# Images 0 to 3 combined among the last expert tiles, and the pair sum of the others done by TensorE as it turns them

## Chip, cores and metric

The kernel runs on one core of a Trainium2 chip. The metric is the device time of one execution in microseconds (us); the median of the runs is compared.

## The reference, cut to what matters

The input is 16 images of 128 channels by 28 x 28 places. A convolution block and a spiking attention block come first. Their result `t` has 16 x 784 = 12,544 tokens of 128 channels, and then a mixture of experts is added:

```python
top_vals, top_idx = jax.lax.top_k(flat @ Wr, 2)        # flat: layer norm of t, 12544 x 128
top_w = softmax(top_vals)
gates = zeros(N, 8).at[arange(N)[:, None], top_idx].add(top_w)
for e in range(8):
    hdn = gelu(flat @ W1[e] + b1[e])                   # 128 -> 512
    out = out + gates[:, e:e+1] * (hdn @ W2[e] + b2[e])  # 512 -> 128
x = from_tokens(t + out)                               # back to channels x places
```

So every token has two chosen experts, and its result is the sum of two gated expert rows and of `t`, turned from token rows into channel rows.

## The kernel before, in words

**First stage (to about 390 us).** Images go through convolution, attention and routing. For each token two rows are sent to a table in HBM, sorted by expert. The sum `t` of each image stays in SBUF (`t2_all`).

**Tile loop (to about 696 us).** The table is worked off in 105 tiles of 256 rows (`TILES`). Every engine runs its own loop over the tiles; semaphores order them.

- SP (`load_tile`, issue L464 and L467) loads tile t turned (`xrt`, four slots) and its routing fields. It waits until the hidden layer of tile t-4 is done, so a load is issued three tiles ahead of its use.
- TensorE runs `hidden(t + 2)` (L943, 24 products into `pair_b` or `pair_c`, in two halves) and then `output(t)` (L957 and L960, into `pair_d`).
- ScalarE runs `gelu` (L1152), which reads the PSUM half and writes a float32 copy `g` in SBUF (in `seen_g`), and `high_half` (L1159), which rounds `g` to float16.
- VectorE runs `gated` (L1656: output times gate into `y`), every fourth tile `fields` (L1631 to L1634), and `split` (L1640: `g` minus its float16 half, two pieces a tile). `output(t)` waits for both pieces of `split(t)`. `hidden(t + 2)` waits for the two `gelu` halves of tile t, which have then left the PSUM pair free.
- POOL (`store_tile`, L678) scatters the 256 gated rows of a tile to the table `expert_rows` in HBM, by two indirect DMAs of 128 rows. `y` has room for 16 tiles, so POOL may run late.

**Combination (from about 696 us).** For each of 16 images:

- SP loads the two expert rows of every token (`load_y`, L481, 784 KB), into 8 buffers in turn. The first six are issued after the last `load_tile` and after a wait for the stores of tiles 0 to 87 (`KNOWN`), which hold all rows of images 0 to 12. Images 13 to 15 wait for all stores.
- VectorE adds the two rows (`sum_rows`, L1697).
- TensorE turns the sum by seven transposes (`turn_sum`, L995).
- VectorE adds `t` (`add_rows`, L1703) and writes `o` (four buffers, in `seen_g`, over `g`).
- ScalarE's queue sends `o` to the output (L1192, 392 KB an image). `add_rows(i)` waits until the output of image i-4 has landed.

Of the kernel before, what the change touches and what calls it, by code (L numbers as in the profile page):

```python
# [33 lines left out]
P = 128  # L34
# [67 lines left out]
def build(nc, a, out):  # L102
# [7 lines left out]
    with ExitStack() as ctx:  # L110
# [61 lines left out]
        def part(words):  # L172
# [50 lines left out]
        xrt = sb("xrt", [P, DEEP, 2, TILE], F16)  # L223
        g = seen_g[:, 0:4 * FC * TILE].bitcast(F32).rearrange("p (u f k) -> p u f k", u=2, f=FC)
        ghl = xb_x1[:, 0:2 * FC * TILE].bitcast(F16).rearrange("p (u h k) -> p u h k", u=2, h=2)
# [11 lines left out]
        fetched = p1_area[0:TT, :].rearrange("p (u t k d) -> p u t k d", u=FETCHED, t=NT, k=2)  # L237
        later = w1_place[0:TT, 0:(ROW_BUFFERS - FETCHED) * 2 * NT * P].rearrange("p (u t k d) -> p u t k d", u=ROW_BUFFERS - FETCHED, t=NT, k=2)
        ysum = w2_place[0:TT, 0:SUM_DEEP * NT * P].rearrange("p (u t d) -> p u t d", u=SUM_DEEP, t=NT)
        o = seen_g[:, 0:2 * SUM_DEEP * L].bitcast(F32).rearrange("p (u l) -> p u l", u=SUM_DEEP)  # L240
# [16 lines left out]
            "dest_ready", "y_ready", "y_copied", "stored_0", "stored_1", "stored_2", "stored_3",  # L257
            "yl_loaded_0", "yl_loaded_1", "yl_loaded_2", "yl_loaded_3", "yl_loaded_4", "yl_loaded_5", "yl_loaded_6", "yl_loaded_7", "ysum_ready", "yt_ready", "o_ready", "out_0", "out_1", "out_2", "out_3",
        )}

        def rows_of(i):

            b = i % ROW_BUFFERS
            return fetched[:, b] if b < FETCHED else later[:, b - FETCHED]

# [79 lines left out]
        def mean_place(n):  # L345

            pair = (pb, pc, pd, pd)[n // 2]
            return pair[:, n % 2 * BANK:(n % 2 + 1) * BANK]

        def score_pair(t):  # L350
# [4 lines left out]
        def _(sp):  # L355
# [121 lines left out]
            def load_y(i):  # L477

                if some(i + 1 - ROW_BUFFERS):
                    sp.wait_ge(S["ysum_ready"], i + 1 - ROW_BUFFERS)  # L480
                sp.dma_start(rows_of(i).rearrange("p t k d -> p (t k d)"), y_img[i]).then_inc(S[f"yl_loaded_{i % ROW_BUFFERS}"], 16)  # L481

# [18 lines left out]
            for b in range(STORE_BATCHES):  # L501
                sp.wait_ge(S[f"stored_{b}"], 32 * store_uses(b, KNOWN))
            for i in range(FETCHED):
                load_y(i)
            sp.wait_ge(S["h_ready"], 2 * TILES)
            for i in range(FETCHED, EARLY_IMAGES):
                load_y(i)
            for b in range(STORE_BATCHES):
                sp.wait_ge(S[f"stored_{b}"], 32 * store_uses(b))
            for i in range(EARLY_IMAGES, IMAGES):  # L510
                load_y(i)


# [179 lines left out]
        def _(pe):  # L693
# [240 lines left out]
            def hidden(t):  # L934
                w0 = experts[t] * HID
                hp, slot = (pb, pc)[t % 2], t % DEEP

                if some(2 * (t - 1)):
                    pe.wait_ge(S["g_ready"], 2 * (t - 1))
                pe.wait_ge(S[f"xrt_loaded_{slot}"], 16 * (t // DEEP) + 16)  # L940
                for f in range(FC):
                    for m, (wp, xp) in enumerate(((0, 0), (0, 1), (1, 0))):
                        last = T.matmul(hp[:, f * TILE:(f + 1) * TILE], w1[:, wp, bass.ds(w0 + f * P, P)],  # L943
                                        xrt[:, slot, xp, :], start=(m == 0), stop=(m == 2))
                    if f % GELU_HALF == GELU_HALF - 1:
                        last.then_inc(S["h_ready"], 1)
# [19 lines left out]
            def take_experts(t, count):  # L966
# [3 lines left out]
                experts.update(zip(range(t, t + count), table(mybir.EngineType.PE, tile_w, t, count, E - 1)))  # L970

            take_experts(0, TAKE)
# [17 lines left out]
            def turn_sum(i):  # L990
                if some(i + 1 - SUM_DEEP):
                    pe.wait_ge(S["o_ready"], i + 1 - SUM_DEEP)
                pe.wait_ge(S["ysum_ready"], i + 1)
                for t in range(NT):
                    last = T.transpose(psum[i % SUM_DEEP][:, t * P:t * P + TT], ysum[:, i % SUM_DEEP, t, :], ident[0:TT, 0:TT])  # L995
                last.then_inc(S["yt_ready"], 1)

            for i in range(IMAGES):
                turn_sum(i)
# [3 lines left out]
        def _(act):  # L1003
# [137 lines left out]

            def half_of(tensor, t, h):
                return tensor[:, t % 2, GELU_HALF * h:GELU_HALF * (h + 1), :].rearrange("p f k -> p (f k)")

            def gelu(t):
                hp = (pb, pc)[t % 2]
                if some(2 * (t - 1)):
                    act.wait_ge(S["ghl_ready"], 2 * (t - 1))
                for h in range(2):

                    act.wait_ge(S["h_ready"], 2 * t + h + 1)
                    A.activation(half_of(g, t, h), hp[:, h * BANK:(h + 1) * BANK], ACT.Gelu, scale=1.0 / WSCALE).then_inc(S["g_ready"], 1)  # L1152

            def high_half(t):
                if some(t - 1):
                    act.wait_ge(S["y_ready"], t - 1)
                for h in range(2):
                    act.wait_ge(S["g_ready"], 2 * t + h + 1)
                    A.activation(ghl[:, t % 2, 0, h * 2 * TILE:(h + 1) * 2 * TILE], half_of(g, t, h), ACT.Copy).then_inc(S["g_hi_ready"], 1)  # L1159

# [28 lines left out]

            for i in range(IMAGES):  # L1190
                act.wait_ge(S["o_ready"], i + 1)
# [6 lines left out]
        def _(dve):  # L1198
# [444 lines left out]
            def gv(t, h):  # L1643
                return g[:, t % 2, 2 * h:2 * h + 2, :].rearrange("p f k -> p (f k)")

# [4 lines left out]
            def gated(t):  # L1650
                slot, (q, half) = t % DEEP, batch_of(t)
                dve.wait_ge(S["y_ready"], t + 1)
                if slot == 0:
                    dve.wait_ge(S["gate_ready"], q + 1)
                b0 = (t % 2) * BANK
                V.tensor_tensor(y[:, t % STORE_DEEP, :, :], pd[:, b0:b0 + 2 * P].rearrange("p (s c) -> p s c", s=2),  # L1656
                                bc_last(share[:, half, slot, :], P), ALU.mult).then_inc(S["y_copied"], 1)

            fields(0, 0)
# [3 lines left out]
            for t in range(TILES):  # L1663
# [29 lines left out]
            def sum_rows(i):  # L1693
                if some(i + 1 - SUM_DEEP):
                    dve.wait_ge(S["yt_ready"], i + 1 - SUM_DEEP)
                dve.wait_ge(S[f"yl_loaded_{i % ROW_BUFFERS}"], 16 * (i // ROW_BUFFERS) + 16)
                V.tensor_tensor(ysum[:, i % SUM_DEEP, :, :], rows_of(i)[:, :, 0, :], rows_of(i)[:, :, 1, :], ALU.add).then_inc(S["ysum_ready"], 1)  # L1697

            def add_rows(i):
                dve.wait_ge(S["yt_ready"], i + 1)  # L1700
                if some(16 * (i // SUM_DEEP)):
                    dve.wait_ge(S[f"out_{i % SUM_DEEP}"], 16 * (i // SUM_DEEP))
                V.tensor_tensor(o[:, i % SUM_DEEP, :].rearrange("p (q t) -> p t q", t=NT), psum[i % SUM_DEEP][:, 0:NT * P].rearrange("p (t k) -> p t k", k=P)[:, :, 0:TT],  # L1703
                                t2_all[:, i * L:(i + 1) * L].rearrange("p (t k) -> p t k", k=TT), ALU.add).then_inc(S["o_ready"], 1)

            dve.wait_ge(S["t2_kept_0"], 32 * PAIRS)
            dve.wait_ge(S["t2_kept_1"], 32 * PAIRS)
            for i in range(SUM_AHEAD):
                sum_rows(i)
            for i in range(IMAGES):  # L1710
                if i + SUM_AHEAD < IMAGES:
                    sum_rows(i + SUM_AHEAD)
                add_rows(i)

# [22 lines left out]
```

## Time and profile before

| what | us |
|---|---|
| runs | 753.41, 750.35, 753.29 (median 753.29) |
| the profiled execution, its own time | 751.24 |
| its span, first to last instruction | 749.5 |
| TensorE busy in the span | 626.6 (84%) |
| VectorE, ScalarE, POOL busy | 571.1, 486.2, 464.6 |

The rows further down come from this one profiled execution. A timeline row gives the start, the duration, the engine, the line, the operation and what it writes and reads; a bracket says how long the engine was idle before and what ended that. "x7" means that seven records are merged in one row; a float32 product makes two records, a float32 transpose one.

### The profile page before, as it was taken

The numbers are of one execution on the slowest core, as the hardware profiler recorded it, in microseconds if no ns is written. First come the engines' busy times: TensorE is split into PE (matmuls) and PEld (weight loads), VectorE is DVE, ScalarE is ACT, GpSimd is POOL, SyncE is SP. The second block draws the span as 40 slices with busy tenths as digits, with TensorE's granted clock in tenths as the row PEclk, the third lists the DMA queues.
The fourth block names the chain that finished last, engine by engine and source line by source line (L and its number), as shares of the span: only waits on it lengthen the run. The fifth ranks groups of instructions, "written<-read, shape, count | busy, mean of one in ns | idle before, by whom it ended". The sixth has DMA issues, their size and how long they took to land.

```text
span 749.5 us, 20954 instructions
## 1 busy us (share of the span) xinstructions
PE 626.6 (84%) x6696; PEld 493.1 (66%) x6696; DVE 571.1 (76%) x1757; ACT 486.2 (65%) x940; POOL 464.6 (62%) x476
## 2 busy tenths in 40 slices
PE   1577879888888898889749899999999999999533
PEld 1244555555555555555529898989999999999423
DVE  6567978999998899999767778656666666666867
ACT  1256757777876677877638777777777777777000
POOL 7000025666666576577777677777777777777720
PEclk9988978999999999999859999999999999999755
DMA  5754484655555555552245344564444454447996
GB/s 142 216 153 127 118 204 127 178 178 163 165 154 162 166 178 179 150 166 95 67 107 97 80 95 95 118 132 90 100 101 93 101 102 95 90 99 195 328 343 263
DMA packets 138771, 108.85 MB, mean 145 GB/s; under 512 B 100339, under 2 KB 121367, under 8 KB 138674
## 3 DMA queue, kind: packets, MB, share of 16 engines
q1 hardware_dynamic: 121874, 75.13, 40.2%
q0 software_dynamic: 13056, 26.02, 11.8%
q10 hardware_dynamic: 3744, 6.43, 2.5%
q8 instruction: 58, 0.95, 0.5%
q14 instruction: 39, 0.32, 0.2%
HBM read 45.26 MB, written 42.85 MB: 118 GB/s over the span
## 4 chain that ended last, share of the span: by engine, by line
PE 45%; DVE 23%; DMA 14%; ACT 6%; issue 5%; SPq 4%; POOL 2%; DVEq 0%; POOLq 0%; ACTq 0%
PE pair_d L960 16%; PE pair_b L943 8%; PE pair_c L943 7%; DMA conv_planes<-conv_y 6%; DMA out<-seen_g 5%; PE pair_a L741 3%; DMA conv_y<-conv_planes 3%; DVE xb_x L1640 3%; DVE p_area L1387 2%; PE pair_c L827 2%; ACT p_area L1051 2%; PE pair_d L957 2%; DVE w L1467 1%; DVE st L1314 1%; SPq L411 1%
## 5 line engine op out<-in xcount | busy, mean ns | idle before, releaser
L678 POOL DMA_INDIRECT expert_rows<-conv_y,dest x210 | 226.6, 1079 | 67.5 <-issue 58.6
L607 POOL DMA_INDIRECT dispatched_rows<-p_area,pos x198 | 198.9, 1005 | 110.3 <-issue 54.4
L960 PE MATMUL pair_d<-w,xb_x 128*128 x2520 | 168.2, 220 | 0.0
L1159 ACT ACTIVATE xb_x<-seen_g 128x512 f16<-128x512 f32 x210 | 120.8, 624 | 61.7 <-PE pair_d L960 59.8
L960 PEld LDWEIGHTS pair_d<-w,xb_x 128*128 128x128 f16 x2520 | 152.3, 98 | 2.5
L1640 DVE TENSOR_TENSOR xb_x<-seen_g,xb_x 128x512 f16<-128x512 f32 x210 | 135.7, 688 | 22.2 <-ACT xb_x L1159 20.2
L1656 DVE TENSOR_TENSOR conv_y<-pair_d,share 128x256 f32<-128x256 f32 x105 | 44.5, 424 | 70.6 <-PE pair_d L960 68.4
L741 PE MATMUL pair_a<-conv_y,p_area 128*32 128x392 f16 x1152 | 64.7, 366 | 20.8 <-DMA conv_y<-conv_planes 15.7
L943 PE MATMUL pair_b<-xrt,w 128*128 128x256 f16 x636 | 79.4, 275 | 2.3 <-issue 2.3
L943 PE MATMUL pair_c<-xrt,w 128*128 128x256 f16 x624 | 78.3, 276 | 0.0
L600 POOL TENSOR_TENSOR conv_y<-conv_y 128x784 f16<-128x784 f32 x16 | 26.0, 1625 | 73.2 <-ACT conv_y L1030 73.0
L943 PEld LDWEIGHTS pair_b<-xrt,w 128*128 x636 | 60.4, 99 | 8.9 <-issue 2.4
L943 PEld LDWEIGHTS pair_c<-xrt,w 128*128 x624 | 59.9, 99 | 6.8
L741 PEld LDWEIGHTS pair_a<-conv_y,p_area 128*32 128x32 f16 x1152 | 29.9, 104 | 42.8 <-issue 27.1
L1152 ACT ACTIVATE seen_g<-pair_b 128x512 f32<-128x512 f32 x106 | 56.7, 585 | 1.7 <-PE pair_b L943 1.1
L1152 ACT ACTIVATE seen_g<-pair_c 128x512 f32<-128x512 f32 x104 | 55.5, 584 | 0.0
L957 PE MATMUL pair_d<-b,two_rows 128*128 x210 | 46.2, 220 | 4.9 <-DVE xb_x L1640 4.5
L1077 ACT ACTIVATE seen_g<-pair_a 112x784 bf16<-112x784 f32 (+2 forms) x48 | 30.6, 638 | 25.6 <-PE pair_a L817 25.1
L1051 ACT ACTIVATE p_area<-pair_b,shift,rstd 112x128 f32<-112x128 f32 x112 | 40.9, 469 | 5.7 <-DVE shift L1348 5.6
L1077 ACT ACTIVATE seen_g<-pair_c 112x672 bf16<-112x672 f32 (+1 forms) x64 | 30.2, 471 | 16.4 <-PE pair_c L817 16.4
L797 PE MATMUL pair_c<-w_t,p_area 128*112 128x128 f32 x224 | 29.6, 286 | 10.8 <-ACT p_area L1067 9.5
L797 PEld LDWEIGHTS pair_c<-w_t,p_area 128*112 128x112 f32 x224 | 26.7, 185 | 16.7 <-DVE p_area L1387 14.2
(264 smaller groups left out, 1094.1 us busy)
## 6 DMA issues: line engine op xcount, KB each, us to landing
conv_y<-conv_planes SPq DMA_DIRECT2D x64, 225.0 KB, 3.9
xb_x<-in_x SPq DMA_DIRECT2D x32, 392.0 KB, 4.4
p_area<-expert_rows SPq DMA_DIRECT2D x12, 784.0 KB, 17.0
conv_planes<-conv_y SPq DMA_DIRECT2D x32, 225.0 KB, 5.1
t_all<-p_area SPq DMA_DIRECT2D x16, 392.0 KB
out<-seen_g ACTq DMA_DIRECT2D x16, 392.0 KB, 9.4
t_all<-in_L_ffn_W SPq DMA_DIRECT2D x16, 256.0 KB, 4.9
expert_rows<-conv_y,dest POOLq DMA_INDIRECT x210
```

The costliest lines, as they stand in the source:

```text
L607: pool.indirect_dma_start(xs, bass.IndirectOffsetOnAxis(ap=pos[0:m, u, t, k:k + 1].bitcast(U32), axis=0), rows[0:m, u, t, :].bitcast(U32), ...
L678: pool.indirect_dma_start(ys, bass.IndirectOffsetOnAxis(ap=dest[:, place, slot, s:s + 1].bitcast(U32), axis=0), y[:, t % STORE_DEEP, s, :] ...
L741: last = T.matmul(pa[g * GROUP_CHANNELS:(g + 1) * GROUP_CHANNELS, h * BANK:h * BANK + HALF], tap_w[:, g, tap, :], stacked_rows[:, u, g, ky ...
L797: last = T.matmul(pc[0:TT, t * P:(t + 1) * P], xt[:, t * TT:(t + 1) * TT], w_t[:, 2, :], start=True, stop=True)
L943: last = T.matmul(hp[:, f * TILE:(f + 1) * TILE], w1[:, wp, bass.ds(w0 + f * P, P)], xrt[:, slot, xp, :], start=(m == 0), stop=(m == 2))
L957: T.matmul(dst, two_rows[:], b2[:, bass.ds(c0, P)], start=True, stop=False)
L960: last = T.matmul(dst, ghl[:, t % 2, gp, f * TILE + s * P:f * TILE + (s + 1) * P], w2[:, wp, bass.ds(w0 + f * P, P)], start=False, stop=(f ...
L1051: last = A.activation(xn[:, t, :], pb[0:TT, t * P:(t + 1) * P], ACT.Identity, scale=rstd[0:TT, t:t + 1], bias=shift[0:TT, t:t + 1])
L1077: A.activation(seen[:, t * L + t * TT:(t + 1) * L], score_pair(t)[0:TT, 0:L - t * TT], ACT.Sign).then_inc(S["seen_ready"], 1)
L1152: A.activation(half_of(g, t, h), hp[:, h * BANK:(h + 1) * BANK], ACT.Gelu, scale=1.0 / WSCALE).then_inc(S["g_ready"], 1)
L1159: A.activation(ghl[:, t % 2, 0, h * 2 * TILE:(h + 1) * 2 * TILE], half_of(g, t, h), ACT.Copy).then_inc(S["g_hi_ready"], 1)
L1640: V.tensor_tensor(ghl[:, t % 2, 1, h * 2 * TILE:(h + 1) * 2 * TILE], gv(t, h), ghl[:, t % 2, 0, h * 2 * TILE:(h + 1) * 2 * TILE], ALU.subt ...
```

## The change

- `gelu` writes its result back into the PSUM half that it read (`hidden_half`), and `high_half` and `split` read it there; `g` in SBUF is gone. So `hidden(t)` now waits, half by half, for `split(t - 2)` in place of `gelu(t - 2)`.
- SP issues the row loads of images 0 to 6 among its tiles 96 to 102, after a wait for the stores of tiles 0 to 87 at its tile 96. Eleven row buffers take the place of eight.
- Images 0 to 3 are combined inside the tile loop: `sum_rows(i)` on VectorE at the end of tile 92 + 3i, `turn_sum(i)` on TensorE after the output of tile 94 + 3i, `add_rows(i)` on VectorE in two parts, at the ends of tiles 94 + 3i (4 of the 7 columns) and 96 + 3i (3 of 7). SP sends their outputs.
- For images 4 to 15 VectorE's `sum_rows` is gone. TensorE makes 14 float32 products an image in place of 7 transposes: each of the two row blocks times the identity, accumulated in PSUM.

```diff
-FETCHED, ROW_BUFFERS = 6, 8
-SUM_DEEP, SUM_AHEAD = 4, 2
+FETCHED = 6
+ROW_BUFFER_OF = (0, 1, 2, 3, 4, 5, 6, 0, 1, 2, 3, 7, 8, 9, 10, 4)
+SUM_DEEP, SUM_HALF = 4, 4
+COMBINED, COMBINE_AT, COMBINE_EVERY = 4, 92, 3
+FETCH_AT, FETCHED_AMONG = 96, 7
...
# SP, in its loop over the tiles, and after it
                 load_tile(t)
+                if t == FETCH_AT:
+                    for b in range(STORE_BATCHES):
+                        sp.wait_ge(S[f"stored_{b}"], 32 * store_uses(b, KNOWN))
+                if FETCH_AT <= t < FETCH_AT + FETCHED_AMONG:
+                    load_y(t - FETCH_AT)
+            for i in range(COMBINED):
+                sp.wait_ge(S["yt_ready"], i + 1)
+                load_y(FETCHED_AMONG + i)
+                if i < COMBINED - 1:
+                    store_out(i)
...
# TensorE
-                if some(2 * (t - 1)):
-                    pe.wait_ge(S["g_ready"], 2 * (t - 1))
                 for f in range(FC):
+                    if f % GELU_HALF == 0 and some(2 * (t - 2) + 1):
+                        pe.wait_ge(S["ghl_ready"], 2 * (t - 2) + f // GELU_HALF + 1)
...
+                    for t in range(NT):
+                        for k in range(2):
+                            last = T.matmul(sum_pair(i)[:, t * P:t * P + TT], rows_of(i)[:, t, k, :], ident[0:TT, 0:TT], start=(k == 0), stop=(k == 1))
...
                 output(t)
+                for i in range(COMBINED):
+                    if t == COMBINE_AT + COMBINE_EVERY * i + 2:
+                        turn_sum(i)
...
# ScalarE
-                    A.activation(half_of(g, t, h), hp[:, h * BANK:(h + 1) * BANK], ACT.Gelu, scale=1.0 / WSCALE).then_inc(S["g_ready"], 1)
+                    A.activation(hidden_half(t, h), hidden_half(t, h), ACT.Gelu, scale=1.0 / WSCALE).then_inc(S["g_ready"], 1)
...
# VectorE
-                    V.tensor_tensor(ghl[:, t % 2, 1, h * 2 * TILE:(h + 1) * 2 * TILE], gv(t, h),
+                    V.tensor_tensor(ghl[:, t % 2, 1, h * 2 * TILE:(h + 1) * 2 * TILE], hidden_half(t, h),
...
+                    if t == at:
+                        sum_rows(i)
+                    if t == at + 2:
+                        add_rows(i, 0, SUM_HALF)
+                    if t == at + 4:
+                        add_rows(i, SUM_HALF, NT)
```

## Rows read from the trace of the kernel before

**Rows 1.** Windows of 10 us after the tile loop, and one inside it (columns in the first line).

```profile
core 0: us, PE busy (x) PEld busy (x) DVE busy (x) ACT busy (x) POOL busy (x), PEclk, DMA share, GB/s
655.00:682.00 27.00, 27.00 (x367) 25.34 (x365) 17.13 (x41) 20.31 (x41) 21.18 (x20) 1.00 0.47 97
690.00:700.00 10.00, 7.47 (x101) 6.54 (x98) 7.15 (x15) 2.91 (x7) 7.87 (x8) 1.00 1.02 309
...
720.00:730.00 10.00, 3.79 (x18) 2.81 (x16) 7.23 (x6) 0.00 (x0) 0.00 (x0) 0.50 1.03 354
```

**Rows 2.** Chain of waits after the tile loop: start us, us, what.

```profile
712.75 14.88 DMA out<-seen_g
```

**Rows 3.** TensorE's last tiles in order of time (start us, us, engine, line).

```profile
686.58 1.47 PE L943 MATMUL pair_c<-xrt,w 128*128 128x256 f16 x12
...
689.34 1.47 PE L943 MATMUL pair_b<-xrt,w 128*128 128x256 f16 x12
...
695.61 0.83 PE L960 MATMUL pair_d<-w,xb_x 128*128 x12
```

**Rows 4.** VectorE in one late tile and in the combination, in order of time.

```profile
684.68 1.30 DVE L1640 TENSOR_TENSOR xb_x<-seen_g,xb_x 128x512 f16<-128x512 f32 x2 [0.24 <-ACT xb_x L1159]
...
704.65 1.58 DVE L1703 TENSOR_TENSOR seen_g<-pair_c,t_all 128x784 f32<-128x784 f32 x1
706.08 1.07 DVE L1697 TENSOR_TENSOR w<-p_area 112x896 f32<-112x896 f32 x1
...
745.08 1.54 DVE L1703 TENSOR_TENSOR seen_g<-pair_d,t_all 128x784 f32<-128x784 f32 x1
```

**Rows 5.** Float32 work of TensorE in the first stage, in order of time.

```profile
292.45 1.40 PE L850 MATMUL pair_d<-wr_c,p_area 128*128 128x8 f32 x12
293.71 0.37 PE L852 MATMUL pair_d<-wr_c,rests 128*128 128x8 f32 x2
...
302.32 0.89 PE L771 MATMUL pair_b<-ident,p_area 112*128 112x112 f32 x7
303.14 0.88 PE L741 MATMUL pair_a<-conv_y,p_area 128*32 128x392 f16 x16
305.00 1.75 PE L797 MATMUL pair_c<-w_t,p_area 128*112 128x128 f32 x14 [0.98 <-ACT p_area L1067]
306.59 0.19 PE L860 MATMUL pair_b<-chosen,before 128*128 128x64 bf16 x1
```

**Rows 6.** TensorE around 416 us, after its longest wait, in order of time.

```profile
416.72 0.23 PE L957 MATMUL pair_d<-b,two_rows 128*128 x1 [1.99 <-DVE xb_x L1640]
416.83 1.39 PE L960 MATMUL pair_d<-w,xb_x 128*128 x12
...
419.40 2.10 PE L943 MATMUL pair_c<-xrt,w 128*128 128x256 f16 x12
```

**Rows 7.** TensorE's waits in the tile loop: us in total, times, longest us.

```profile
PE pair_d L957 <- DVE xb_x L1640: 3.8, 5, 2.0
```

**Rows 8.** Groups by line and shape: VectorE over PSUM and SBUF, 512 wide.

```profile
L1461 DVE TENSOR_TENSOR t_all<-t_all,pair_d 127x512 f32<-127x512 f32 x4 | 2.7, 684 | 3.1 <-PE pair_d L723 3.1
```

**Rows 9.** POOL's stores of expert rows, in order of time.

```profile
668.59 1.05 POOL L678 DMA_INDIRECT expert_rows<-conv_y,dest  x1 [0.30 <-issue]
...
704.88 0.97 POOL L678 DMA_INDIRECT expert_rows<-conv_y,dest  x1 [0.30 <-issue]
706.16 1.83 POOL L678 DMA_INDIRECT expert_rows<-conv_y,dest  x1 [0.30 <-issue]
```

**Rows 10.** VectorE's gated copy of tile 87.

```profile
650.40 0.42 DVE L1656 TENSOR_TENSOR conv_y<-pair_d,share 128x256 f32<-128x256 f32 x1 [0.23 <-PE pair_d L960]
```

**Rows 11.** SP's queue: the last load of tile 96, the first of tile 97.

```profile
658.77 0.38 SPq L467 DMA_DIRECT2D fld<-dispatched_rows  x1
660.07 2.02 SPq L464 DMA_TRANSPOSE xrt<-dispatched_rows  x1
```

**Rows 12.** DMA issues from 655 to 682 us: KB each, median us to landing.

```profile
p_area<-expert_rows SPq DMA_DIRECT2D x1, 784.0 KB, 6.6
```

More of the change, by code:

```diff
@@ L970, in take_experts, with turn_sum @@
                 experts.update(zip(range(t, t + count), table(mybir.EngineType.PE, tile_w, t, count, E - 1)))
+            def turn_sum(i):
+                if i <= COMBINED:
+                    if some(i):
+                        pe.wait_ge(S["o_ready"], i)
+                elif i < COMBINED + SUM_DEEP:
+                    if i == COMBINED + SUM_DEEP - 1:
+                        pe.wait_ge(S["y_copied"], TILES)
+                else:
+                    pe.wait_ge(S["o_ready"], i + 1 - SUM_DEEP)
+                if i < COMBINED:
+                    pe.wait_ge(S["ysum_ready"], i + 1)
+                    for t in range(NT):
+                        last = T.transpose(sum_pair(i)[:, t * P:t * P + TT], rows_of(i)[:, t, 0, :], ident[0:TT, 0:TT])
+                else:
+                    pe.wait_ge(S[f"yl_loaded_{ROW_BUFFER_OF[i]}"], loads_of(i))
+                    for t in range(NT):
+                        for k in range(2):
+                            last = T.matmul(sum_pair(i)[:, t * P:t * P + TT], rows_of(i)[:, t, k, :], ident[0:TT, 0:TT], start=(k == 0), stop=(k == 1))
+                last.then_inc(S["yt_ready"], 1)
             take_experts(0, TAKE)
@@ L987, in _ @@
                 output(t)
[L990 to L998, printed above, removed]
+                for i in range(COMBINED):
+                    if t == COMBINE_AT + COMBINE_EVERY * i + 2:
+                        turn_sum(i)
+            for i in range(COMBINED, IMAGES):
                 turn_sum(i)
@@ L1187, in _ @@
                     gate_tanh(q, half)
-            for i in range(IMAGES):
+            for i in range(COMBINED, IMAGES):
                 act.wait_ge(S["o_ready"], i + 1)
@@ L1657, in gated, with sum_rows, add_rows, combine_early @@
                                 bc_last(share[:, half, slot, :], P), ALU.mult).then_inc(S["y_copied"], 1)
+            def sum_rows(i):
+                dve.wait_ge(S[f"yl_loaded_{ROW_BUFFER_OF[i]}"], loads_of(i))
+                V.tensor_tensor(rows_of(i)[:, :, 0, :], rows_of(i)[:, :, 0, :], rows_of(i)[:, :, 1, :], ALU.add).then_inc(S["ysum_ready"], 1)
+            def add_rows(i, t0, t1):
+                if t0 == 0:
+                    dve.wait_ge(S["yt_ready"], i + 1)
+                    if some(16 * (i // SUM_DEEP)):
+                        dve.wait_ge(S[f"out_{i % SUM_DEEP}"], 16 * (i // SUM_DEEP))
+                last = V.tensor_tensor(o[:, i % SUM_DEEP, :].rearrange("p (q t) -> p t q", t=NT)[:, t0:t1], sum_pair(i)[:, 0:NT * P].rearrange("p (t k) -> p t k", k=P)[:, t0:t1, 0:TT],
+                                       t2_all[:, i * L:(i + 1) * L].rearrange("p (t k) -> p t k", k=TT)[:, t0:t1], ALU.add)
+                if t1 == NT:
+                    last.then_inc(S["o_ready"], 1)
+            def combine_early(t):
+                if t == COMBINE_AT:
+                    dve.wait_ge(S["t2_kept_0"], 32 * PAIRS)
+                    dve.wait_ge(S["t2_kept_1"], 32 * PAIRS)
+                for i in range(COMBINED):
+                    at = COMBINE_AT + COMBINE_EVERY * i
+                    if t == at:
[4 more added lines that the diff above has]
+                        add_rows(i, SUM_HALF, NT)
             fields(0, 0)
@@ L1690, in _ @@
                     gate(q, half)
[L1693 to L1713, printed above, removed]
+                combine_early(t)
+            combine_early(TILES)
+            for i in range(COMBINED, IMAGES):
+                add_rows(i, 0, NT)
 _INS = ["x"] + ["L0_conv_" + n for n in ("dw_w", "dw_b", "bn1_g", "bn1_b", "bn1_m", "bn1_v", "pw_w", "pw_b", "bn2_g", "bn2_b", "bn2_m", "bn2_v")] \
```

52 lines of the change are left out of this document (28 added, 24 removed).

## The prediction

> **What bounds the kernel now.** I read the windows first: which engine is full in which stretch, then the clock and the DMA share. In the tile loop TensorE is busy all the time (27.00 of 27.00 us) at the full granted clock, with the DMA engines at 0.47. After the loop this turns round: the DMA share is 1.02 to 1.03, TensorE does under 4 us of work in ten, and its granted clock falls to 0.50, the 1.2 GHz level [rows 1]. Next the chain: its long pieces after the loop are three waits for output transfers, the longest 14.88 us [rows 2]. So there are two stages with two limits: a tile loop set by TensorE, in which 0.53 of the DMA time is unused, and a combination set by transfers. The loop's last product ends at 695.61 + 0.83 = 696.44 us [rows 3]. To the end of the span (749.5 us) that leaves **53.1 us** for the combination.
>
> **The change, part by part.** The sum is made against the profiled execution: 751.24 us, with a span of 749.5. It is 2.05 us below the median of the runs, so I work out the difference and subtract that from 753.29.
>
> *Transfers.* Seven of 16 row loads and the first outputs move into the loop. Of the tail's transfers, about six loads and 13 outputs are left: at the tail's 309 GB/s [rows 1] a load of 803 KB takes 2.6 us and an output of 401 KB 1.3 us, together 33 us. That is less than TensorE's new work below, so TensorE is late next.
>
> *Turning with the sum (images 4 to 15).* Seven transposes become 14 float32 products, 28 records an image. No row shows this shape, so I bound it. Records that hardly stream and are set by loading 128 columns came at (293.71 - 292.45) / 12 = 0.105 us; records that stream 128 columns at (306.59 - 305.00) / 14 = 0.114; transposes of 112 columns, with the same operands, at (303.14 - 302.32) / 7 = 0.117 [rows 5]. The new ones load 128 and stream 112, nearest to the first: I take 0.11, that is 3.08 us an image and **37.0 us** for twelve (35.3 to 39.3). VectorE's 1.54 us an image [rows 4] lies beside it. After the loop's last output TensorE first waits for image 3's second part, since image 4 uses its PSUM pair: start of the gated copy 0.2, copy 0.42 [rows 10], three sevenths of the 1.54 us add with its fixed part 0.75, together about 1.4 us. Behind the last product come one add (1.54 and 0.2 to start) and what now follows the last add, 749.5 - 745.08 - 1.54 = 2.9 us [rows 4]. New tail: 1.4 + 37.0 + 1.7 + 2.9 = 43.0 us, **10.1 us less**.
>
> *Combining images 0 to 3 in the loop.* Each turn takes TensorE 0.82 us [rows 5], on the path: 3.3 us. VectorE has the time: in a tile its pieces are 0.42 and 1.30 us of 2.76 (689.34 - 686.58) [rows 3, 4, 10], and one pair sum (1.07) or half add (0.96 or 0.75) follows. But turn i waits for the second half add of image i - 1, which VectorE reaches only behind that tile's gated copy and split; with the pair sum of the tile before pushing it by some 0.3 us I get waits of 0.3 us (image 1) and 0.7 (image 2, whose tile has the fields too). At the end, from the end of output 101, VectorE runs copy, split, pair sum 3, copy, fields, split, half add: 6.2 us. TensorE is through its products after 4.2 us, waits 2.0, turns image 3 (0.8) and does the last output (1.45): 8.6 us where it was 696.44 - 689.34 = 7.1. So 3 x 0.82 + 1.0 + 1.5 = **5.0 us more**.
>
> *GELU in place.* ScalarE and VectorE now read or write PSUM. For the split the nearest row is a VectorE subtraction of 512 columns of PSUM from SBUF: 684 ns [rows 8], against 1.30 / 2 = 0.65 for a piece now; I take no change. ScalarE writing to PSUM stands in no row; ScalarE is idle for a quarter of the loop [rows 1], so between 0.3 us less and 0.3 more a tile it is covered; I take zero. The new wait of `hidden` for the split: the split that starts at 684.68 has its first piece ready at 685.33, and the product that would wait for it starts at 686.58 [rows 3, 4]. That cover is 1.25 us; VectorE's insertions use 0.3 to 0.5 of it. It fails only where VectorE is already late: five waits, 3.8 us in all [rows 7]. There `hidden` waits too, which before ran in the shadow of the wait, for about 0.5 us more; but VectorE or a field load, not TensorE, sets the time in these places, so they don't add up: **0.5 us more** (0 to 2.5).
>
> *The clock.* After its longest wait, 1.99 us, TensorE ran slower for some 4 us: 12 products took 1.39 us for 0.83, 12 others 2.10 for 1.47 [rows 3, 6]. Both output halves and the hidden layer together, that cost 1.8 us. The 2.0 us wait near the end is like it: **1.8 us more** (0 to 1.8). After that the products follow each other without gaps, as in the first stage.
>
> *POOL and SP.* SP's wait at tile 96 stands ahead of the tile loads that feed TensorE, so it counts. Before, tile 87's rows are ready at 650.82 us but POOL begins to store them at 668.59: 17.8 us late [rows 9, 10]. A store takes 0.97 us and 0.30 between two, so 2.55 us a tile, less than TensorE's 2.76: POOL should catch up, and doesn't. Why: a store that began at 706.16, inside VectorE's pass over two SBUF tiles (706.08 to 707.15), took 1.83 us; one that began inside a pass over PSUM and SBUF (704.65) took 0.97 [rows 4, 9]. The split is now of the first kind, and becomes one of the second. Gaining 0.21 us a tile over some 71 tiles, POOL makes up about 15 us and is 3 us late at tile 87: stores issued by 656.4, and landed before or just after SP asks, at 659.2 [rows 11]. The first row load takes 6.6 us [rows 12]; VectorE wants it near 666.6. So zero.
>
> The Trainium skill, "SBUF — State Buffer", section "Who interferes with whom", has two sentences here: a VectorE instruction with two SBUF inputs contends with a GpSimd instruction that reads SBUF, but a tensor-tensor pass should not hold up descriptor generation (marked there as inferred). By the second, the split never delayed POOL and the lag stays. The rows of 1.83 and 0.97 us speak against that; rival one is what it would give.
>
> **Sum:** -10.1 + 5.0 + 0.5 + 1.8 = **-2.8 us**, that is 748.4 on the profiled run, and **750.5** from the median.
>
> **Rivals.**
> 1. *SP's wait for stored rows (slower).* If POOL stays 17.8 us late, SP stands until 668.59 + 2.6, about 671, not 659.2. The first row load lands at 677.6; VectorE stands at pair sum 0 until then, and after 1.07 + 0.42 + 0.2 + 0.65 us the hidden layer of tile 97 starts at 680.0, not 670.0 (689.34 - 7 x 2.76). Price 10 us: **760.5**. It decides from a lag of about 9 us on. For it: the lag has held over the loop. Against it: the two rows above.
> 2. *Turned tiles late behind row loads.* Both go through SP's queue. A tile uses 0.47 x 2.76 = 1.3 us of DMA time, a load 2.6: 3.9 us in a period of about 3.05 with the turns. After seven, 3.9 + 6 x 0.85 = 9 us are queued, with some 2 us to land, against 670.0 - 660.07 = 9.9 us from a tile's load to its use. Price 0 to 5 us, say 3: **753.5**, no change.
> 3. *Half clock through the whole tail.* 12 images at twice 3.08 us: 37 us more, **787.5**. Against it: unbroken float32 work, which the first stage did at the full rate.
> 4. *TensorE better than taken.* 0.105 a record, no fall of the clock, no early waits: 1.7 + 1.8 + 0.5 less, **746.5**.
>
> **Chances and range.** A difference of 0.5%, 3.8 us, is about what a measurement can tell from none. The forecast with rival 4 as its lower end has 0.72 (its own range 745 to 755), rival 1 0.12, rival 2 0.12, rival 3 0.04. Of the 0.72 the part below 749.5 is 0.42, as the forecast lies only 1 us above that line and its bounds reach 4 below; 0.28 is no change, 0.02 slower. Rival 2 gives 0.07 and 0.05. So faster 0.42, same 0.35, slower 0.23. The range, with run scatter of 1.5 us, is 744.5 to 757.5, which leaves out rivals 1 and 3 at their full price.
>
> **What would show it.** Right: the granted clock stays at 1.00 in most of the tail; 28 records an image in about 3.1 us back to back, and output waits gone from the chain; stores no slower than about 1 us, POOL done a few us after the last tile; the end of the loop at 702 to 704 us. Wrong: TensorE idle before the hidden layer of tiles 97 to 104 with a load or the split as releaser; float32 records of 0.2 us; splits well over 0.7 us; the chain in the tail still on transfers.

## The result, and the profile after

The changed kernel took 756.75 us (median of 20 runs, 751.70 to 764.93) against 750.09 for the kernel before, run beside it (20 runs, 742.22 to 760.27). The ratio is 1.0104, 95% interval 1.0076 to 1.0132: about 1% slower. The forecast was 750.5 us, and most likely faster or no change. That 756.75 still lies inside the range (to 757.5) is luck: the forecast started from a median of three runs, 753.29, and the 20 runs of the same kernel give 3.2 us less. Taken from 750.09, the same sum gives 747.3 and a range to 754.3. What follows is about why the sign was wrong. The ratios are of fast runs: a run more than 1.5% above the fastest of its kernel counts as slow and is left out, and so are the stage times of `behind_fields_half_tail`, whose profile was taken in such a run.

The profiled execution took 754.19 us with a span of 752.5, and 751.24 and 749.5 before. Two events divide it: the first product of the tile loop and the last. In time order, TensorE, the loop's first product before, then after:

```profile
388.59 2.74 PE L943 MATMUL pair_b<-xrt,w 128*128 128x256 f16 x12 [2.27 <-issue]
```

```profile
386.70 2.74 PE L975 MATMUL pair_b<-xrt,w 128*128 128x256 f16 x12 [2.25 <-issue]
...
708.21 0.83 PE L992 MATMUL pair_d<-w,xb_x 128*128 x12
710.22 3.38 PE L1021 MATMUL pair_a<-ident,p_area 112*128 112x112 f32 x28 [1.18 <-DVE seen_g L1706]
713.44 3.29 PE L1021 MATMUL pair_b<-ident,p_area 112*128 112x112 f32 x28
...
744.70 3.29 PE L1021 MATMUL pair_d<-ident,p_area 112*128 112x112 f32 x28
```

Before, the loop ended at 696.44 [rows 3]. So:

| profiled execution, us | before | after | difference | forecast |
|---|---|---|---|---|
| before the loop | 388.59 | 386.70 | -1.9 | 0 |
| tile loop | 307.85 | 322.34 (to 708.21 + 0.83) | **+14.5** | +7.3 |
| combination behind it | 53.06 | 43.46 | **-9.6** | -10.1 |
| span | 749.5 | 752.5 | +3.0 | -2.8 |

The change does not touch what comes before the loop; the 1.9 us there are taken as scatter between executions. The combination did what was forecast. The loop lost twice as much as forecast, and there lies the error.

The same windows as [rows 1], after:

```profile
655.00:682.00 27.00, 23.91 (x302) 22.27 (x300) 16.20 (x35) 15.88 (x34) 15.57 (x16) 0.94 1.01 219
...
712.00:722.00 10.00, 10.00 (x92) 10.00 (x91) 4.80 (x3) 0.00 (x0) 0.69 (x1) 1.00 1.02 276
...
732.00:742.00 10.00, 10.00 (x92) 10.00 (x91) 5.00 (x4) 0.00 (x0) 0.00 (x0) 1.00 0.55 215
```

Behind the loop TensorE is now full at a granted clock of 1.00 (it was under four tenths, at 0.50), and it bounds that stage. In the loop's end TensorE has lost 3.1 of 27 us, and the DMA share has gone from 0.47 to 1.01. The chain of waits names what it stood for, the landing of two field loads:

```profile
668.23 7.32 DMA fld<-dispatched_rows
...
684.42 8.02 DMA fld<-dispatched_rows
```

VectorE waits for these fields, and TensorE for VectorE's split behind them (VectorE first, then TensorE, in order of time):

```profile
675.65 0.17 DVE L1672 TENSOR_TENSOR mine<-fld,tile_expert 128x8 f32<-128x8 f32 x1 [4.77 <-DMA fld<-dispatched_rows]
...
692.54 0.17 DVE L1672 TENSOR_TENSOR mine<-fld,tile_expert 128x8 f32<-128x8 f32 x1 [4.34 <-DMA fld<-dispatched_rows]
```

```profile
676.95 1.60 PE L975 MATMUL pair_b<-xrt,w 128*128 128x256 f16 x12 [3.09 <-DVE xb_x L1681]
...
681.11 1.73 PE L975 MATMUL pair_c<-xrt,w 128*128 128x256 f16 x12
...
693.84 1.48 PE L975 MATMUL pair_b<-xrt,w 128*128 128x256 f16 x12 [3.34 <-DVE xb_x L1681]
```

`fields(q)` runs on VectorE between the gated copy of tile 4q - 2 and the split of tile 4q. SP issues the field load of the batch's last tile, 4q + 3, at the earliest when the hidden layer of tile 4q - 1 is done. VectorE wants it some 3 us later: 668.23 to 675.65 - 4.77 = 670.88 is 2.65 us, and 684.42 to 692.54 - 4.34 = 688.20 is 3.78. Among row loads of 784 KB those 3 KB took 7 to 8 us. SP's queue around the first of them, the row load of image 2 and the field load:

```profile
666.16 0.47 SPq L498 DMA_DIRECT2D p_area<-expert_rows  x1
...
668.23 0.40 SPq L486 DMA_DIRECT2D fld<-dispatched_rows  x1
```

The two waits of TensorE are 6.4 us. The products behind the first were slow, at a mean granted clock of 0.65, that is in part at the lower of its two levels: from one hidden layer to the next it took 681.11 - 676.95 = 4.16 us, not 2.76, and the next was 0.26 late too, together 1.7. Behind the second wait, the longer one, the granted clock was 1.00 and the first twelve products took the usual 1.48 us.

### The profile page after: what moved, and what is told of

It reads as the page before. It is cut to its first block, busy times and chain, and to the rows that moved or that the text cites. A ratio compares the mean times of both kernels' runs of the same rounds, so it can differ in the third digit from the quotient of the medians.

```text
span 752.5 us, 21336 instructions
## 1 busy us (share of the span) xinstructions
PE 644.3 (86%) x6948; PEld 514.2 (68%) x6948; DVE 559.9 (74%) x1749; ACT 480.8 (64%) x940; POOL 443.1 (59%) x476
## 3 DMA queue, kind: packets, MB, share of 16 engines
q0 software_dynamic: 13056, 26.02, 11.9%
## 4 chain that ended last, share of the span: by engine, by line
PE 46%; DVE 26%; DMA 9%; ACT 6%; issue 5%; SPq 4%; POOL 2%; DVEq 0%; POOLq 0%; ACTq 0%
PE pair_d L992 15%; PE pair_b L975 8%; PE pair_c L975 7%; DMA conv_planes<-conv_y 4%; DMA fld<-dispatched_rows 3%; PE pair_a L773 3%; DVE xb_x L1681 2%; DVE p_area L1428 2%; DMA conv_y<-conv_planes 2%; DVE st L1348 2%; PE pair_c L859 2%; ACT p_area L1098 1%; DVE st L1355 1%; PE pair_d L989 1%; DVE w L1508 1%
## 5 line engine op out<-in xcount | busy, mean ns | idle before, releaser
L710 POOL DMA_INDIRECT expert_rows<-conv_y,dest x210 | 204.8, 975 | 86.8 <-issue 55.9
L1200 ACT ACTIVATE xb_x<-pair_b 128x512 f16<-128x512 f32 x106 | 57.6, 595 | 39.0 <-PE pair_d L992 38.2
L1200 ACT ACTIVATE xb_x<-pair_c 128x512 f16<-128x512 f32 x104 | 56.5, 596 | 31.5 <-PE pair_d L992 29.5
L1681 DVE TENSOR_TENSOR xb_x<-pair_b,xb_x 128x512 f16<-128x512 f32 x106 | 68.1, 683 | 10.4 <-ACT xb_x L1200 10.4
L1681 DVE TENSOR_TENSOR xb_x<-pair_c,xb_x 128x512 f16<-128x512 f32 x104 | 66.9, 685 | 9.2 <-ACT xb_x L1200 8.6
L1193 ACT ACTIVATE pair_b<-pair_b 128x512 f32<-128x512 f32 x106 | 58.0, 589 | 3.0 <-PE pair_b L975 2.8
L1193 ACT ACTIVATE pair_c<-pair_c 128x512 f32<-128x512 f32 x104 | 56.4, 584 | 1.1 <-PE pair_c L975 1.0
L1124 ACT ACTIVATE seen_g<-pair_a 112x784 bf16<-112x784 f32 (+2 forms) x48 | 30.6, 638 | 21.9 <-PE pair_a L849 21.5
```

Source lines behind the costliest of these rows:

```text
L710: pool.indirect_dma_start(ys, bass.IndirectOffsetOnAxis(ap=dest[:, place, slot, s:s + 1].bitcast(U32), axis=0), y[:, t % STORE_DEEP, s, :] ...
L1124: A.activation(seen[:, t * L + t * TT:(t + 1) * L], score_pair(t)[0:TT, 0:L - t * TT], ACT.Sign).then_inc(S["seen_ready"], 1)
L1193: A.activation(hidden_half(t, h), hidden_half(t, h), ACT.Gelu, scale=1.0 / WSCALE).then_inc(S["g_ready"], 1)
```

## The experiments

Each ratio is to runs of the kernel before on the same chip.

| run | ratio to before, 95% interval | loop, us | behind it, us |
|---|---|---|---|
| before (profiled) | 1 | 307.85 | 53.06 |
| the change | 1.0104 [1.0076, 1.0132] | 322.34 | 43.46 |
| rows_behind_fields | 0.9959 [0.9921, 0.9997] | 311.91 | 43.46 |
| rows_on_act | 1.0262 [1.0188, 1.0335] | 327.56 | 43.38 |
| gelu_in_place_alone | 1.0029 [0.9983, 1.0075] | 310.64 | 53.27 |
| tail_on_vector | 0.9989 [0.9944, 1.0034] | 321.05 | 38.04 |
| spare_loads_each_tile | 1.0149 [1.0075, 1.0222] | 319.73 | 53.87 |
| spare_loads_behind_fields | 1.0021 [0.9972, 1.0070] | 311.16 | 54.64 |
| behind_fields_vector_tail | 0.9899 [0.9827, 0.9971] | 313.71 | 39.11 |
| behind_fields_half_tail | 0.9869 [0.9794, 0.9943] | - | - |
| before_fields_first | 0.9965 [0.9934, 0.9997] | 306.58 | 51.58 |
| fields_first | 0.9937 [0.9895, 0.9980] | 315.56 | 43.45 |
| fields_first_vector_tail | 0.9851 [0.9805, 0.9896] | 315.68 | 36.40 |
| fields_first_spaced_rows | 0.9871 [0.9820, 0.9921] | 311.46 | 37.91 |

Loop and rest are of the one profiled execution of each run (first hidden product to the end of the last output product, and from there to the end of the span), the ratio is of all its runs. Whole runs of one kernel scatter by 1 to 2%. The loop scatters less: three pairs of runs with the same loop (the change and `tail_on_vector`, `rows_behind_fields` and `behind_fields_vector_tail`, `fields_first` and `fields_first_vector_tail`) differ in it by 1.3, 1.8 and 0.1 us, so a difference under 2 us is read as none.

### Where the row loads stand in SP's queue

```diff
-                if FETCH_AT <= t < FETCH_AT + FETCHED_AMONG:
-                    load_y(t - FETCH_AT)
+                for i in ROWS_AT.get(t, ()):
+                    load_y(i)
...
+ROWS_AT = {95: (0,), 96: (1,), 99: (2,), 100: (3,), 103: (4,), 104: (5, 6)}
```

> The changed kernel, with the row loads of images 0 to 6 issued by SP at its tiles 95, 96, 99, 100, 103 and 104 (one, one, one, one, one, two) in place of one at each of the tiles 96 to 102, so that none stands ahead of the last two tile loads of a batch of four. Queue theory (the fields of tiles 99 and 103 land 7.3 and 8.0 us after their issue because row loads are ahead of them, and cost 3.1 and 3.3 us of TensorE time and 1.9 us of slower clock): fields land in under 4 us there, both stalls go, 6 to 9 us less than the changed kernel, ratio to the kernel before 0.998 to 1.003. In-place theory (the time goes to the hidden layer's new wait for the split and to VectorE's added passes): the stalls stay whatever the order of the loads, ratio 1.008 to 1.012.

The loop fell from 322.34 to 311.91 us, more than the 6 to 9 us that the queue theory gave. VectorE's waits for fields from 600 to 720 us, the change first, then this run:

```profile
DVE mine L1672 <- DMA fld<-dispatched_rows: 10.6, 5, 4.8
```

```profile
DVE mine L1673 <- DMA fld<-dispatched_rows: 1.5, 3, 0.7
```

The longest is 0.7 us, no longer 4.8, although the transfers stayed as dense (columns as in [rows 1], in a window of 40 us):

```profile
650.00:690.00 40.00, 39.99 (x539) 37.70 (x537) 31.44 (x62) 29.03 (x58) 27.14 (x28) 1.00 1.01 218
```

TensorE is full (39.99 of 40 us) at a DMA share of 1.01. So the early fetch need not cost field stalls, and the place of the loads decides. (They are also spread over ten tiles here and not seven; `fields_first`, below, leaves them at one a tile.) But is it their place in SP's queue, or in time? Next, the seven loads left SP's queue for ScalarE's, which issues them in its own loop, behind the work of its tiles 93 to 99.

```diff
+                if FETCH_AT - 5 <= t < FETCH_AT - 5 + FETCHED_AMONG:
+                    n = t - FETCH_AT + 5
+                    act.dma_start(rows_of(n).rearrange("p t k d -> p (t k d)"), ys.rearrange("(b p r) d -> b p (r d)", b=IMAGES, p=TT)[n]).then_inc(S[f"yl_loaded_{ROW_BUFFER_OF[n]}"], 16)
```

> The changed kernel, with the seven row loads among the tiles issued from ScalarE's queue, one behind each of its tiles 91 to 97, in place of SP's. The same bytes at about the same times, on another queue. If it is the order within SP's queue that delays the fields: they land in under 4 us, both stalls go, 6 to 9 us less than the changed kernel. If it is the DMA engines' time, whatever the queue: fields still land after 6 us or more and 0 to 3 us are saved. In-place theory: no difference from the changed kernel.

```profile
670.96 12.30 DMA fld<-dispatched_rows
...
692.68 7.54 DMA fld<-dispatched_rows
```

The kernel got slower still, its loop 5.2 us longer, where 0 to 3 us less were expected. With SP's queue free of row loads, a field load took 12.30 us to land. So the delay needs no row load ahead of it in that queue: large loads in flight from another queue do it as well. By what mechanism inside the DMA engines is not shown.

### The disputed cost by itself

The kernel before, with seven spare loads of 784 KB from `x` into the row buffers, long before these are needed.

```diff
                 load_tile(t)
+                for n in SPARE_LOADS.get(t, ()):
+                    sp.dma_start(fetched[:, n % FETCHED].rearrange("p t k d -> p (t k d)"), a["x"].rearrange("(n b) c h w -> n (b c h w)", b=2)[n].rearrange("(p r) -> p r", p=TT)).then_inc(S["spare_loads"], 16)
...
+SPARE_LOADS = {t: (t - 64,) for t in range(64, 71)}
```

> The kernel before, with nothing of the change in it but the disputed cost by itself: seven loads of 784 KB from the input x into the row buffers (which nobody needs at that time), one behind each of the tiles 64 to 70 in SP's queue, as the changed kernel has its row loads behind tiles 96 to 102. Theory (a field load queued among such loads takes 7 to 8 us and is wanted after some 3): two waits of VectorE for fields of 4 to 5 us each appear, at the batches of tiles 68 and 72, TensorE then waits some 3 us each time, and runs slow for a while behind it; the span grows by 6 to 9 us and the time by about 1%. Rival (the stalls of the changed kernel come from the combination in the loop, which makes VectorE late, and the loads only show beside it): no wait for fields above 1 us here, span and time as before within 1.5 us.

In order of time, VectorE's waits, then TensorE's:

```profile
584.91 0.17 DVE L1635 TENSOR_TENSOR mine<-fld,tile_expert 128x8 f32<-128x8 f32 x1 [4.56 <-DMA fld<-dispatched_rows]
...
602.35 0.17 DVE L1635 TENSOR_TENSOR mine<-fld,tile_expert 128x8 f32<-128x8 f32 x1 [6.40 <-DMA fld<-dispatched_rows]
```

```profile
586.81 0.29 PE L961 MATMUL pair_d<-b,two_rows 128*128 x1 [2.85 <-DVE xb_x L1644]
...
604.25 0.28 PE L961 MATMUL pair_d<-b,two_rows 128*128 x1 [4.69 <-DVE xb_x L1644]
```

Nothing of the change is in this kernel, and the two stalls are there, at the places that the theory gives, the first of the size it gives and the second larger. The loop is 11.9 us longer, the time 1.5%, more than the 6 to 9 us and 1% expected.

```diff
-SPARE_LOADS = {t: (t - 64,) for t in range(64, 71)}
+SPARE_LOADS = {63: (0,), 64: (1,), 67: (2,), 68: (3,), 71: (4,), 72: (5,), 75: (6,)}
```

> The same seven loads of 784 KB in the kernel before, but behind tiles 63, 64, 67, 68, 71, 72 and 75, so that none is in SP's queue in the two tiles ahead of a batch's last fields. Theory: no wait for fields above 1 us, span as before within 1.5 us, although the same 5.6 MB pass through the same engines in about the same time. Rival (the bytes themselves cost the time, by whatever order): the span grows by as much as in the run with one load behind each tile.

The windows of the two, this one second, have nearly the same rate of bytes (230 and 216 GB/s), but TensorE 32.16 and 39.91 us busy of 40:

```profile
565.00:605.00 40.00, 32.16 (x406) 29.58 (x404) 19.04 (x43) 22.66 (x46) 31.17 (x30) 0.94 1.09 230
```

```profile
565.00:605.00 40.00, 39.91 (x544) 37.54 (x541) 25.73 (x55) 30.49 (x60) 31.10 (x30) 1.00 1.06 216
```

One field load was late by 2.65 us here as well, and TensorE by 0.94, so the bound of 1 us was too tight. It was issued 0.43 us ahead of a spare load (602.74) and still took 5.28 us, so a place behind the last fields is no guarantee:

```profile
602.31 5.28 DMA fld<-dispatched_rows
```

The profiled loop is 3.3 us longer than before, but the ratio can't be told from 1. So the bytes alone cost at most a small part of the time.

### The parts of the change

GELU in place without anything else (the hunks of `hidden`, `gelu`, `high_half` and `split` on the kernel before):

```diff
-                    A.activation(half_of(g, t, h), hp[:, h * BANK:(h + 1) * BANK], ACT.Gelu, scale=1.0 / WSCALE).then_inc(S["g_ready"], 1)
+                    A.activation(hidden_half(t, h), hidden_half(t, h), ACT.Gelu, scale=1.0 / WSCALE).then_inc(S["g_ready"], 1)
```

> The kernel before with one part of the change: GELU writes back into PSUM, and the hidden layer waits for the split of two tiles earlier. Queue theory: TensorE waits 1 to 3 us more in the loop's first quarter and nothing later; POOL's stores take 0.98 us at most on average and end a few us after the last tile in place of 21 us after it, so that the last three images load earlier; ratio 0.993 to 1.003. In-place theory: 5 to 8 us more in the loop, ratio 1.005 to 1.010.

No difference that the runs can tell (1.0029, interval on both sides of 1); in the profiled loop it is 2.8 us more. TensorE's waits from 383 to 712 us, before ([rows 7] has a shorter window) and in this run:

```profile
PE pair_d L957 <- DVE xb_x L1640: 4.5, 6, 2.0
```

```profile
PE pair_b L947 <- DVE xb_x L1641: 5.6, 5, 2.1
...
PE pair_d L961 <- DVE xb_x L1641: 1.1, 2, 0.8
```

What it does to POOL stands alone here. The group of stores, the kernel before and this one:

```profile
L678 POOL DMA_INDIRECT expert_rows<-conv_y,dest x210 | 226.6, 1079 | 67.5 <-issue 58.6
```

```profile
L682 POOL DMA_INDIRECT expert_rows<-conv_y,dest x210 | 205.6, 979 | 76.2 <-issue 59.8
```

A store is 0.1 us shorter, and POOL ends 5.6 us after the loop in place of 21.9, with GELU's result in PSUM as the only edit. That edit takes an operand of VectorE's split out of SBUF, but also what ScalarE's `gelu` wrote and `high_half` read. The trace of before has a store that separates them: the one at 693.32 us took 1.19 us, inside the last split (692.98 to 694.27), when the last GELU had ended at 691.66. Next, the change with its pair sums of images 4 to 15 back on VectorE and seven transposes an image:

```diff
-            for i in range(COMBINED, IMAGES):
-                add_rows(i, 0, NT)
+            for i in range(COMBINED, COMBINED + 2):
+                sum_rows(i)
+            for i in range(COMBINED, IMAGES):
+                if i + 2 < IMAGES:
+                    sum_rows(i + 2)
+                add_rows(i, 0, NT)
```

> The changed kernel, with the pair sums of images 4 to 15 on VectorE again (1.07 us each, two images ahead) and seven transposes an image on TensorE. If TensorE's products are what bounds the changed tail (12 x 3.13 = 37.5 us): VectorE's 12 x (1.07 + 1.56) = 31.6 us or the transfers' 33 us bound it now, 2 to 5 us less than the changed kernel. If transfers bound both: no difference within 1 us. The loop and its two stalls are the same in both.

The combination falls from 43.46 to 38.04 us, and the time with it (0.9989 for 1.0104), while the loop keeps its stalls. The two longest pieces of the chain behind the loop are waits for output transfers again, and TensorE is at half clock, with VectorE busy for 9.53 of 10 us:

```profile
706.32 13.43 DMA out<-seen_g
...
721.42 9.70 DMA out<-seen_g
```

```profile
720.00:730.00 10.00, 4.94 (x23) 4.02 (x24) 9.53 (x8) 0.00 (x0) 0.00 (x0) 0.50 1.01 270
```

So what shortened the combination is that seven loads and four images had moved into the loop, not the products with the identity. These made it 5.4 us longer than it need be: a bound of 43 us in place of one of 38.

### Versions that beat both

The edits of `rows_behind_fields` and `tail_on_vector` together:

> The changed kernel with the row loads behind the last fields of a batch, and with the pair sums of images 4 to 15 on VectorE and seven transposes an image on TensorE, as before the change. Theory (the two gains have different places and add up: the loop's end near 699 us, the tail 38 us): span about 737 us, some 5 us under the run with the rows behind the fields alone, time about 0.988 of the kernel before. Rival (in that run the tail is bounded by transfers, and since fewer of them ran in the loop's end or all start later, the tail gets longer as the loop gets shorter): span 740 to 743, no better than either alone.

0.9899 (interval below 1), 742.2 us of span where 737 was forecast: the loop was 313.71 and not 311.9, the combination 39.11 and not 38, and the rest of the difference lies ahead of the loop. The two gains add up, less some 3 us.

> As the run before it, but only images 5, 7, 9, 11 and 13 are summed on VectorE; the other seven of images 4 to 15 are summed by TensorE's products with the identity. Theory A (with all sums on VectorE the tail is set by output transfers, some 33 us of them and more with their waits): relieving VectorE gives nothing, span within 1.5 us of the run with all sums on VectorE. Theory B (there VectorE's 2.6 us an image, or the half clock of the transposes, sets it): TensorE needs 7 x 3.13 + 5 x 1.2 = 28 us, VectorE 12 x 1.54 + 5 x 1.07 = 24 us, and the tail falls from 38 to about 35 us, the span to some 734 us.

```diff
+SUMMED = (5, 7, 9, 11, 13)
...
-                if i < COMBINED:
+                if i < COMBINED or i in SUMMED:
```

Here some images keep the products. The ratios are 0.9869 and 0.9899, each within the other's interval: no gain that the runs can tell, which fits theory A and does not settle it.

Since the place behind the last fields is no guarantee (5.28 us, above), the next runs give the fields more time. The four field loads of a batch are issued with its first tile:

```diff
-                sp.dma_start(fld[:, half, slot, :, :], xs16[bass.ds(tiles_at[t], TILE), 2 * P:ROW].bitcast(F32).rearrange("(s p) c -> p s c", p=P)).then_inc(S[f"fields_{half}"], 16)
+                for n in range(min(DEEP, TILES - t) if slot == 0 else 0):
+                    sp.dma_start(fld[:, half, n, :, :], xs16[bass.ds(tiles_at[t + n], TILE), 2 * P:ROW].bitcast(F32).rearrange("(s p) c -> p s c", p=P)).then_inc(S[f"fields_{half}"], 16)
```

> The kernel before, with one change in SP's queue: the four field loads of a batch (3 KB each) are issued together behind the first tile of the batch, not one behind each tile. VectorE wants all four about three tiles later, so the last of them has some 11 us to land and not 3. Theory (the fields are late because the last one is issued only 3 us ahead of its use): the waits of VectorE for fields, 6 to 7 us over the loop of before, fall under 2 us, TensorE's waits for the split fall from 4.5 to 1 or 2 us, and the span is 2 to 5 us shorter. Rival (the waits of the loop's beginning come from VectorE's other work, the fields only show beside them): waits of TensorE and span as before within 1.5 us.

In the kernel before, the waits for fields (6.5 us in all there) are gone entirely, but TensorE's waits for the split are not:

```profile
PE pair_d L958 <- DVE xb_x L1641: 4.2, 6, 2.0
```

The rival holds here: the waits early in the loop were not for fields. The loop is 1.3 us shorter, the time 0.35% less.

> The changed kernel with the same edit, its row loads still one behind each of the tiles 96 to 102. Theory (it is the short time between a field load and its use that makes the row loads cost anything): no wait for fields above 1 us near the row loads although these stand where they stood; TensorE's two waits of 3.1 and 3.3 us and the slow stretch behind the first are gone, the loop is 8 to 12 us shorter, span 741 to 744. Rival (row loads delay the turned tiles or the stores too, and TensorE would next wait for those): the loop is less than 4 us shorter, and TensorE waits for xrt.

In the changed kernel VectorE has no wait for fields left, with the row loads where the change puts them, one a tile: it was the short slack of the fields, and not how close the row loads stand, that made the field stalls. The loop is 6.8 us shorter, less than the 8 to 12 expected (span 748.9 for 741 to 744), since the next late thing appears, the turned tiles:

```profile
681.61 1.48 PE L976 MATMUL pair_b<-xrt,w 128*128 128x256 f16 x12 [0.49 <-DMA xrt<-dispatched_rows]
686.65 1.48 PE L976 MATMUL pair_c<-xrt,w 128*128 128x256 f16 x12 [1.98 <-DMA xrt<-dispatched_rows]
694.48 1.48 PE L976 MATMUL pair_c<-xrt,w 128*128 128x256 f16 x12 [0.90 <-DMA xrt<-dispatched_rows]
```

That is 3.4 us in three waits, and the expectation's rival is half right.

The same with the edit of `tail_on_vector`:

> The same, with the pair sums of images 4 to 15 on VectorE and seven transposes an image, as before the change. Theory: the loop as in the run before it, the tail 38 to 39 us instead of 43.5 and bounded by output transfers (waits of 9 to 15 us for them, granted clock 0.50 to 0.6), so a span of 736 to 739 us and a time of about 0.985 of the kernel before. Rival (a shorter loop only moves more transfers into the tail): a tail of 42 us or more, no better than the run before it.

0.9851, as expected, with 36.40 us behind the loop, less than the 38 to 39 expected. The span, 742.1, is above the 736 to 739 expected: the loop stays at 315.68 with 3.6 us in three waits for turned tiles, and one of these took 10.76 us to land. Last, the row loads behind every second tile:

```diff
+ROWS_AT = {95: (0,), 97: (1,), 99: (2,), 101: (3,), 103: (4,), 104: (5, 6)}
```

> The run with the fields of a batch first and the pair sums of images 4 to 15 on VectorE, with one more edit: row loads behind tiles 95, 97, 99, 101 and 103 and two behind tile 104, that is every second tile and not every tile. Theory (with the fields out of the way the turned tiles are what the row loads delay: 2.6 us of transfers for a load and 1.3 for a tile do not fit into a tile's 2.76 us, but do into two tiles): TensorE's waits for xrt, 3.1 us in the run before, are gone, the loop is 3 to 4 us shorter (312 us from the first hidden product to the last output product), the tail stays at 37 to 39 us, span 737 to 740, time about 0.98 of the kernel before. Rival (the clock after any wait or the combination itself makes the loop long): the loop stays at 315 us, the time within 0.3% of the run before.

There is no wait for xrt any more and the loop is 311.46 us, 4.2 shorter, as the theory says; behind it, 1.5 us came back. The ratios, 0.9871 and 0.9851, each to its own runs of before, lie within each other's intervals: the time is no better, as the rival says. So both are 1.3 to 1.5% faster than the kernel before, and by the ratios (divided by 1.0104) 2.3 to 2.5% faster than the changed one; which of them is better stays open.

## Why the prediction was wrong

**The step that failed: the slack of SP's loads.** The prediction's sum has no term for what the row loads do to the other loads of SP; rival 2 puts it at "0 to 5 us, say 3", for the turned tiles alone. The mechanism of rival 2 was right: loads of 2.6 us and tiles of 1.3 us in periods of 3.05 queue up. But it held the queued 9 us against 9.9 us "from a tile's load to its use", the slack of the turned tiles, and took that for the slack of all that SP loads. The fields of a batch's last tile go behind the turned tile in the same queue, and had 2.65 and 3.78 us. The cost was 6.4 us of waits and 1.7 of slow products, 8.1 us that the sum did not have; `rows_behind_fields`, without them, has a loop 10.4 us shorter (1.4 of this are the early waits, below, 0.6 a shorter wait at a turn). The edit that takes the short slack away leaves 3.4 us for the turned tiles (`fields_first`), which is what rival 2 had priced, and row loads at every second tile leave none (`fields_first_spaced_rows`): right mechanism, wrong victim. The trace of before had the clue, in a row that was not read for this, VectorE's waits over the whole kernel:

```profile
DVE mine L1631 <- DMA fld<-dispatched_rows: 6.5, 7, 2.4
```

Even with the DMA engines half idle the fields came late seven times. `before_fields_first` shows that this cost little then; but a load that is late in a quiet stretch has no slack in a full one.

**The tail: right.** 43.46 us for 43.0: 1.18 before image 4 (1.4 forecast), 3.13 us an image, that is 0.112 a record (0.11), 2.9 behind the last add (2.9). TensorE bounds it, as forecast, and the rival of half clock fell: 1.00 throughout. What the prediction did not ask is how short the tail gets without the products, by the early fetch and the four images in the loop; `tail_on_vector` says 38 us, with output transfers as its longest waits.

**Combining in the loop, GELU in place, clock: priced too high.** With the field stalls gone (`rows_behind_fields`) the loop is 4.1 us longer than before; 5.0 + 0.5 + 1.8 = 7.3 was forecast. In the changed kernel, the waits at the turns of images 2 and 3 were 0.59 and 1.33 us (forecast 0.7 and 2.0), and none was seen at image 1 (0.3). No slow products followed the 1.33 us, so the 1.8 us for the clock were not due there; the change paid as much behind the first field stall (1.7), and next to nothing behind the second. The early waits were larger than the term taken for them: 5.8 us in the changed kernel where 3.6 stood before (both from 384 to 500 us), 2.2 us more for a term of 0.5 (0 to 2.5), though `rows_behind_fields` shows 4.4 with the same code there, so that part of it is scatter.

**POOL: right in its result.** The prediction held that VectorE's pass over two SBUF tiles slows a store, from two rows [rows 9]. Not each such store is slow: one that began at 703.61, 0.03 us ahead of a pass from 703.64 to 704.73, took 0.97 us, and in the loop from 600 to 694 us about every second store took 1.05 to 1.43, the others 0.97. POOL's stores after:

```profile
L710 POOL DMA_INDIRECT expert_rows<-conv_y,dest x210 | 204.8, 975 | 86.8 <-issue 55.9
```

POOL ends 3.7 us after the loop (711.72 + 0.98 - 709.04; before 717.33 + 0.97 - 696.44 = 21.9), and SP issues its first row load at 659.72 us without standing at its wait. Rival 1 fell. The second of the two sentences of the Trainium skill, "SBUF — State Buffer", section "Who interferes with whom", has it that a tensor-tensor pass would not hold up descriptor generation. The rows speak against it and for the first sentence: 1079 against 979 ns for a store with GELU in place, and 1.19 us for the store inside the last split of before, after the last GELU.

**Time.** The profiled pair differs by 2.95 us, the medians by 6.7 and the ratio by 1.04%: the profiled execution of the change is one of its faster ones, and its first stage happened to end 1.9 us early. Whether the field stalls are longer in slower executions is not shown.

## What to carry to other kernels

When transfers are moved beside a loop, list every load that the loop issues and how long before its use each is issued; the shortest slack decides, not that of the largest or best-known load. A few KB took 5 to 12 us here among transfers of 784 KB, from either queue that was tried, so issue small loads a batch early, which here cost nothing. And try the parts of a change alone: here moving loads and four images into the loop was worth 15 us behind it (53.06 to 38.04) for about 4 in it (`rows_behind_fields`), and the new way of summing took 5 of them back.

## What the runs showed of the hardware that was not expected

- Field loads of 3 KB that were waited for took 5.28 to 12.30 us to land while loads of 784 KB were in flight, and the longest was with these on another engine's queue.
- SP's own instruction that starts a turned tile takes 1.20 us for most tiles, but up to 2.23 us in the kernel before, where the DMA share is 0.47 in [rows 1], and up to 3.14 us in `rows_on_act`; what is queued behind it starts later too.
- TensorE kept a granted clock of 1.00 through 37 us of gapless float32 products. In the tail of before, groups of seven transposes with waits between them took 0.89 us at first and 1.54 us from the fifth on, at a granted clock of 0.50.
- Moving these operands to PSUM changed almost nothing in the engines' own times: ScalarE's GELU of 512 columns took 584 to 589 ns from PSUM back into PSUM and 584 to 585 ns into SBUF, VectorE's split 683 to 685 ns with one operand in PSUM and 688 ns with both in SBUF (means over all tiles, after and before).
